# A graph network on one core: first propagation hop as a pass of its own

## The reference

```python
x = _layernorm(x + _L0_gnn_ref(...))   # two mean aggregations over the edges, and an MLP
x = _layernorm(x + _L1_gnn_ref(...))   # a message per edge (edge features), batch norm, SiLU, mean
x = _layernorm(x + _L2_gnn_ref(...))   # h = x @ W + b; out[dst] += h[src] * attention[edge]
x = _layernorm(x + _L3_gnn_ref(...))
# _L3_gnn_ref, K = 3 hops:
deg = segment_sum(ones, dst) + 1;  dinv = rsqrt(deg);  norm = dinv[src] * dinv[dst]
h = x
for _ in range(K):
    h = segment_sum(norm[:, None] * h[src], dst)     # self loops included
return h @ W + b
```

## Time and profile before

| | us |
|---|---|
| median of 3 runs without the profiler | 7859.46 (7859.25 to 7867.06) |
| span of the profiled execution | 9014.9 |
| edge pass of layer 1, first to last gather issue | 1837.5 to 4242.5 |
| attention pass, first to last gather issue | 4774.6 to 7677.3 |
| last block of layer 2 and of the first hop | 7678 to 7788 |
| second hop | 7788 to 8375 |
| third hop and output | 8375 to 9015 |

### The profile page before, as it was taken

One profiled execution on the slowest core, in us unless ns is written; L12 is line 12 of the kernel. 1 busy time (PEld: TensorE's weight loads), 2 busy tenths in 40 slices (PEclk: granted clock), 3 DMA queues, 4 the chain that ended last, 5 costly groups with the idle time before them and its releaser, 6 DMA issues.

```text
span 9014.9 us, 163525 instructions
## 1 busy us (share of the span) xinstructions
PE 5434.1 (60%) x62971; PEld 4715.0 (52%) x62971; DVE 2921.7 (32%) x5181; ACT 1301.5 (14%) x1613; POOL 3562.5 (40%) x3543
## 2 busy tenths in 40 slices
PE   6999889933333333333652455544555455799999
PEld 6999779922222222222542344433444344799998
DVE  6999521111111111112863323332332332311111
ACT  4777510000000000000750000000000000000000
POOL 2111000056666666666725555555555555000000
PEclk9999899966666666666985666666666766899999
DMA  4444268733333332333831222222222222688887
GB/s 129 183 182 182 86 218 254 247 78 81 87 82 81 82 82 76 82 82 98 251 97 35 56 73 73 75 70 70 73 73 74 76 73 76 196 276 268 264 259 229
DMA packets 559779, 1155.29 MB, mean 128 GB/s; under 512 B 155247, under 2 KB 367217, under 8 KB 546465
## 3 DMA queue, kind: packets, MB, share of 16 engines
q1 hardware_dynamic: 234784, 794.54, 27.5%
q10 hardware_dynamic: 215616, 239.17, 8.2%
q0 software_dynamic: 108896, 114.33, 6.5%
HBM read 898.83 MB, written 248.88 MB: 127 GB/s over the span
## 4 chain that ended last, share of the span: by engine, by line
PE 36%; issue 26%; another core or an unknown queue 15%; DVE 5%; ACT 2%; POOL 1%; DVEq 1%; DMA 1%; ACTq 0%; POOLq 0%; SPq 0%; PEldq 0%
PE banks L859 18%; PE banks L953 10%; PE banks L963 5%; POOL gath L366 1%; DVE oneh L1014 1%; DVE area L1836 1%; DVE area L1894 1%; ACT gath L1383 1%; DVE oneh L1845 1%; ACT banks L1380 1%; PE banks L552 1%; PE banks L540 1%; PE banks L1543 1%; PE banks L1552 0%
## 5 line engine op out<-in xcount | busy, mean ns | idle before, releaser
L366 POOL DMA_INDIRECT gath<-tab_l,idx x3328 | 3145.1, 945 | 3296.1 <-DMA idx<-src_idx 1131.6
L1552 PE MATMUL banks<-area,ones 128*128 128x448 f32 (+1 forms) x1040 | 604.9, 752 | 1248.1 <-DVE area L1836 1050.8
L953 PE MATMUL banks<-area 128*128 128x128 f16 x4802 | 575.4, 247 | 894.6 <-issue 893.9
L1552 PEld LDWEIGHTS banks<-area,ones 128*128 128x128 f32 x1040 | 284.5, 285 | 1536.2 <-issue 1522.1
L953 PEld LDWEIGHTS banks<-area 128*128 128x128 fp8e4 x4802 | 356.6, 107 | 1095.2 <-issue 1091.2
L963 PE MATMUL banks<-oneh,gath 128*64 128x128 f32 x3328 | 581.2, 353 | 411.9 <-DMA gath<-tab_l,idx 349.8
L1836 DVE TENSOR_TENSOR area<-gath,banks 128x448 f32<-128x448 f32 (+1 forms) x256 | 138.6, 583 | 1992.2 <-remote 1194.1
L963 PEld LDWEIGHTS banks<-oneh,gath 128*64 128x64 f32 x3328 | 544.7, 188 | 439.0 <-DMA gath<-tab_l,idx 355.6
L825 ACT CAST wide<-banks 128x784 uint16<-128x784 f32 x784 | 651.5, 859 | 221.9 <-PE banks L782 221.9
L794 PE MATMUL banks<-feat,wide 128*128 128x129 f16 x9604 | 670.6, 220 | 0.3 <-ACT wide L825 0.3
L794 PEld LDWEIGHTS banks<-feat,wide 128*128 128x128 fp8e4 x9604 | 606.2, 97 | 0.5 <-issue 0.5
(11 more groups left out here) (257 smaller groups left out, 6169.2 us busy)
## 6 DMA issues: line engine op xcount, KB each, us to landing
gath<-counts SPq DMA_DIRECT2D x294, 784.0 KB, 4.5
oneh<-counts SPq DMA_DIRECT2D x294, 784.0 KB, 4.5
counts<-wide SPq DMA_DIRECT2D x98, 1568.0 KB, 5.2
gath<-counts ACTq DMA_DIRECT2D x98, 784.0 KB
area<-counts ACTq DMA_DIRECT2D x98, 784.0 KB
area<-edge_feat SPq DMA_DIRECT2D x128, 448.0 KB
gath<-tab_l,idx POOLq DMA_INDIRECT x3328
edge_h<-area ACTq DMA_DIRECT2D x128, 416.0 KB
```

What stands on the lines that cost most here:

```text
L366: pool.indirect_dma_start(out=to[:, h, c, 0:H], out_offset=None, in_=table[:, :], in_offset=bass.IndirectOffsetOnAxis(ap=idx[:, slot, c:c ...
L953: last = T.matmul(to, part_in[u].bitcast(f8)[:, t, s * P:(s + 1) * P], block_rows[:, k % 2, s, :, :].rearrange("p a f -> p (a f)"), start= ...
L1552: ins = T.matmul(bank[n][:, 0:(hi - lo) * H], ones[:, :], src[:, lo:hi, :].rearrange("p c f -> p (c f)"), start=first and lo == 0, stop=la ...
```

## The change

The first hop is taken out of the attention pass. Blocks are still normalised during that pass, but step 15 (ACT's copy of `block_rows`) goes: DVE writes the fp16 pair straight into `parts[0]` in steps 13 and 14. After the pass there are no part products; the hops are three dense passes over `counts`: `parts[0]` to `parts[1]`, `parts[1]` to `parts[0]`, and the last one as before from `parts[0]`. SP loads the whole of `counts` once more, in halves of a tile.

```diff
-        L2_STEPS = 15
+        L2_STEPS = 14
-        def part_load(act, b, j):
-...
-            act.dma_start(part_in[j % 2], counts[j * TB:(j + 1) * TB, :, bass.ds(b * BW, BW)]
-                          .rearrange("t p n -> p t n")).then_inc(c_in[j % 2], 16)
-
-        def high_of_block(k):
-            return lambda b, h: V.tensor_copy(block_rows[:, k % 2, :, 0, :], nod[:, h, 0, :, :])
...
+        def high_of_block(b, h):
+            return V.tensor_copy(tiles(parts_of(0, 0), b), nod[:, h, 0, :, :])
+
+        def low_of_block(b, h):
+            return V.tensor_tensor(tiles(parts_of(0, 1), b), nod[:, h, 0, :, :], tiles(parts_of(0, 0), b), ALU.subtract)
...
             hold(act, p_att.added, groups + 2)
-            l2_steps(act, b, [(1, sums_to_sta), *ln_act(4), (11, keep_resid), (15, keep_block(k))])
-            for j in range(NB):
-                if j + 2 < NB:
-                    part_load(act, b, j + 2)
...
+            l2_steps(act, b, [(1, sums_to_sta), *ln_act(4), (11, keep_resid)])
...
-            def step(b, k, st):
+            def step(b, st):
                 if st == 0:
                     l2_steps(pe, b, [(2, feat_by_node)])
-                elif st <= NB // 2:
-                    for j in (2 * st - 2, 2 * st - 1):
-                        part_product(pe, b, k, j)
...
             pe.wait_ge(p_att.summed, GROUPS + RING)
-            pe.sem_inc(h_mm[1], 1)
-            step(EARLY, EARLY, 0)
-            for j in range(NB):
-                part_product(pe, EARLY, EARLY, j, last_block=True)
...
+            pe.sem_inc(h_mm[1], 4)
+            step(EARLY, 0)
+            pe.wait_ge(l_turn, L2_STEPS * NB + 1)
...
-                elif st <= NB // 2:
-                    for j in (2 * st - 2, 2 * st - 1):
-                        part_added(b, j)
...
-            V.memset(sums_a, 0.0).then_inc(s_pre, 1)
-            V.memset(sums_b, 0.0).then_inc(s_pre, 1)
-            dve.wait_ge(s_pre, 9)
...
-                counts_in(sp, 2, each=store_out)
+                counts_in(sp, 2)
+                counts_in(sp, 3, each=store_out)
...
-                times_counts(pe, 1, 1)
+                times_counts(pe, 1, 0)
                 pe.wait_ge(h_dve[0], H_STEPS[0])
+                times_counts(pe, 2, 1)
+                pe.wait_ge(h_dve[1], H_STEPS[1])
...
-                hop_dve(dve, 1, 0)
+                hop_dve(dve, 1, 1)
+                hop_dve(dve, 2, 0)
```

More of the change, by code:

```diff
@@ L925, in keep_block @@
[L925 to L930, removed]
-            hold(act, p_att.added, groups + 2)
-            l2_steps(act, b, [(1, sums_to_sta), *ln_act(4), (11, keep_resid), (15, keep_block(k))])
-            for j in range(NB):
-                if j + 2 < NB:
-                    part_load(act, b, j + 2)
-                if k == EARLY:
-                    act.wait_ge(f_sc, j + 1)
-                    S.copy(tiles(parts_of(1, 0), j), nod[:, j % 2, 0, :, :]).then_inc(f_hi, 1)
@@ L958, in att_group, with early_act @@
+        def low_of_block(b, h):
+            return V.tensor_tensor(tiles(parts_of(0, 1), b), nod[:, h, 0, :, :], tiles(parts_of(0, 0), b), ALU.subtract)
+        def early_act(act, b, groups):
+            hold(act, p_att.added, groups + 2)
+            l2_steps(act, b, [(1, sums_to_sta), *ln_act(4), (11, keep_resid)])
         def att_group(pe, q, k, h):
@@ L983, in early_pe @@
                     att_group(pe, BEFORE + 2 * EACH * i + s, BEFORE // 2 + EACH * i + s // 2, s % 2)
-                    step(2 * i + s // EACH, s // EACH, s % EACH)
+                    step(2 * i + s // EACH, s % EACH)
             for s in range(EACH - 1):
@@ L987, in early_pe @@
                 att_group(pe, q, q // 2, q % 2)
-                step(EARLY - 1, EARLY - 1, s)
+                step(EARLY - 1, s)
             pe.wait_ge(p_att.summed, GROUPS + RING)
-            pe.sem_inc(h_mm[1], 1)
-            step(EARLY, EARLY, 0)
-            for j in range(NB):
-                part_product(pe, EARLY, EARLY, j, last_block=True)
[L995 to L998, removed]
+            pe.sem_inc(h_mm[1], 4)
+            step(EARLY, 0)
+            pe.wait_ge(l_turn, L2_STEPS * NB + 1)
         def early_dve(dve, l2_work):
@@ L1024, in add, with step @@
                     .then_inc(p_att.added, 1)
[L1026 to L1039 removed]
+            def step(b, st):
                 if st == 0:
[L1041 to L1044 removed]
+                    l2_steps(dve, b, [*l2_work, (13, high_of_block), (14, low_of_block)])
             for q in range(2):
                 place(q, q)
[L1049 to L1051 removed]
             with dve.Fori(0, BEFORE // 2) as i:
@@ L1066, in early_dve @@
                     place(q + 2, q % 2)
-                step(EARLY - 1, EARLY - 1, s)
-            step(EARLY, EARLY, 0)
-            def to_parts(j):
-                dve.wait_ge(f_hi, j + 1)
-                V.tensor_tensor(tiles(parts_of(1, 1), j), nod[:, j % 2, 0, :, :], tiles(parts_of(1, 0), j), ALU.subtract)\
-                    .then_inc(f_lo, 1)
-            for j in range(NB):
-                part_added(EARLY, j)
-                dve.wait_ge(c_ev, 2 * (NB * EARLY + j) + 5)
-                if j >= 2:
-                    dve.wait_ge(f_lo, j - 1)
-                V.scalar_tensor_tensor(nod[:, j % 2, 0, :, :], hop_sums(j), 1.0 / COUNT_UNIT, by_tile(dinv2, j), ALU.mult,
-                                       ALU.mult).then_inc(f_sc, 1)
-                if j > 0:
-                    to_parts(j - 1)
-            to_parts(NB - 1)
-        H_STEPS = [8 * TITERS]
+                step(EARLY - 1, s)
+            step(EARLY, 0)
+        H_STEPS = [8 * TITERS] * 2
         def counts_hold(eng):
@@ L1408, in _ @@
                 edges_to_sums_act(n_win, early=True)
-                with act.Fori(0, EARLY // 2) as i:
-                    for k in range(2):
-                        early_act(act, 2 * i + k, k, BEFORE + EACH * (2 * i + k))
-                early_act(act, EARLY - 1, EARLY - 1, BEFORE + EACH * (EARLY - 1))
-                early_act(act, EARLY, EARLY, GROUPS)
+                with act.Fori(0, EARLY) as b:
+                    early_act(act, b, BEFORE + EACH * b)
+                early_act(act, EARLY, GROUPS)
                 turns(act, d_out, [(7, take_feat), *ln_act(10)], LAST_AT.get, DENSE_PERIOD)
@@ L2048, in _ @@
                 dve.wait_ge(s_fold, 3)
[L2049 to L2050 removed]
+                hop_dve(dve, 1, 1)
+                hop_dve(dve, 2, 0)
+                turns(dve, d_out, [(4, both_parts(3)), (5, last_scaled), (9, lambda b, h: add_resid(b, h, 3)),
                                    *ln_dve(10), (16, result_d)], LAST_AT.get, DENSE_PERIOD)
```

32 lines of the change are left out of this document (3 added, 29 removed).

## The result

| | before | after |
|---|---|---|
| median of 4 runs each | 7859.35 (7853.27 to 7867.06) | 8365.92 (8362.46 to 8367.71) |
| ratio, 95% interval | | 1.0642 (1.0627 to 1.0657) |
| span of the profiled execution | 9014.9 | 8362.4 |

The change makes the kernel 506.6 us slower. The forecast was 8371 (8335 to 8405), 5 us off. In the timed runs the time came out as the sum said. But the profile did not: the recorded execution of the changed kernel has a span 1.8 us shorter than its own time of 8364.17, where a span near 9010 was forecast.

A forecast was written before the change was run, and what follows sets the result against it. Timed runs were taken as bound in both gather passes by POOL's unbroken gather stream; 7859.5 + 587.0 (added pass) - 69.9 (last block's parts) - 5.5 (earlier copy), attention pass 0, gave 8371 us, range 8335 to 8405.

The forecast's parts named there:

- The added pass, +587.0: Third dense pass after the attention pass: same work as the present second hop, nothing else beside it, 587.0 us more.
- D: Rival, slower still: PE gets the low clock for all of the new pass, 440 us more, 8811 us; chance 0.02.
- C: Rival, faster: POOL's waits are real and the change removes all, 826.6 us off, 7544 us; chance 0.03.
- The last block's parts, -69.9: Between step 14 and `fold_bias`: the copy and 14 part products of the last block all go, 69.9 us less.
- the copy, -5.5: Before the last block: ACT's copy of step 1 no longer stands behind part loads in its queue, 5.5 us less.
- The attention pass, 0: Part products, additions and loads beside the attention pass's gathers: hidden under the gather stream in timed runs, 0 us gained.
- the account of waits: Both gather passes: POOL's waits of 1155.5 us match profiled span minus timed median, 1155.4, so timed runs lack them.
- PE "near the edge": Attention pass: PE's work per group, 16.1 us at low clock, barely fits under 16.23 us of gathers; 30 us allowed.
- The profiled span, 9012: Profile after the change: attention pass 514.0 us shorter, its remaining waits still there, span 9012 us, nearly as before.
- Rival B: POOL's waits for PE are real in timed runs too; the change gains 514.0 us, 7857 us, no change; chance 0.07.

The follow-up runs named there:

- the repeat: The kernel before, unchanged, profiled a second time in the first batch; it ran in 7870.74 us with a span of 7868.9.
- third recording of before: The kernel before, unchanged, profiled once more in the second batch on another chip; 7864.49 us, span 7862.6.

## Why the prediction was right, and where it was not

**The added pass, +587.0.** 585.4 in the trace, and 588 between the medians with and without it. Nothing lay beside it, as said: DVE 94.8 us, ACT and POOL none. The granted clock of 0.97 rules out D. The timed runs rule out C: they got longer.

**The last block's parts, -69.9; the copy, -5.5.** In sum -75.4; measured from the last gather to the first hop product, 112.5 us in the repeat (6529.33 to 6641.87) and 28.9 after, so -83.6. With the third recording of before (6529.24 to 6636.94, 107.7 us) it is -78.8. The copy's term was right to 0.2 us (6.2 down to 0.5). The other was 2.7 to 7.6 us too small: the parts take 69.9 us in the recording that it was read from the earlier trace rows, and 77.5 and 72.6 in the two others. That is the spread of this stretch, and it can't be put down to the disturbance.

**The attention pass, 0.** 2084.7 down to 2078.6 us, 6 us. Its working counts 98 groups with parts where there are 91, which a term of 0 does not feel. This was the step on which the sign hung, since 514 or 827 us were on offer in the rows, and it held. The reason given was the account of waits: 1155.5 us of them against 1155.4 us between span and median. The reading that such waits are in no timed run is confirmed by the two more recordings and by leaving out, doubling and tripling the parts. That the account closed to 0.1 us was in part luck: it took 2076.1 us for an unbroken pass, and the repeat has 2079.8 and 2084.7, so that by the repeat the two passes were 1143 us too long, and the whole execution 1146.

**PE "near the edge".** The prediction allowed 30 us for real waits, because 16.1 us of PE's work at low clock would just fit under 16.23. The edge was further off: PE is idle for 6.6 us in an undisturbed group, twice the parts still fit, and three times do not. The estimate took the low clock for all of the work; the granted clock rose with it (the table above).

**The profiled span, 9012.** Wrong. The step that failed is the one from "these waits are not in a timed run" to "so they come with the recording": the forecast carried them over to the profile after, with pitch and backlog of the first twelve groups. They belonged to one execution. One of the signs of being wrong did appear, gathers without any wait in the profile after, which the prediction gave to the mechanism of C; it was the wrong reading of that sign, as two recordings of before have none either. With the Trainium skill's "NOTIFIC — the notification-queue block" (section 7.1) the prediction had named full record queues as what may hold up an engine; no run here shows that to be the cause, and two recordings of the same program without waits show that it is not a constant effect of recording. What disturbed the first one is open; neither of the two further recordings brought it back.

**Rival B and its rule.** It had 0.07 and fell with the part products left out. The Trainium skill's "Runtime: NRT & Kernel Launch" (section on the preamble and postamble), which was named beside it, has a gap between profile and reported time that is the same for every kernel. In every run listed here the span is 1.8 to 2.1 us below the time of the same execution (8362.4 and 8364.17; 7868.9 and 7870.74). So that the gap is nearly constant agrees with these runs, but not its size of 6.2 us, nor its sign: the page has the profile's total as the longer of the two. (The span here runs from the first to the last instruction; whether the page's total is the same measure is not shown.) What the prediction had compared was the span of one execution with the times of others. That the 1155.4 us were a longer execution, and no gap between profile and time, is what a constant gap would suggest; the first recording's own time was not among the numbers, so no run shows it.

**The sum against the medians.** Spans of after and of the repeat differ by 493.5 us. By the starts read above: the attention pass begins 12.3 us earlier (4432.35 against 4444.67, behind unchanged code), is 6.1 shorter, what lies between its last gather and the first hop is 83.6 shorter, the pass adds 585.4, the second hop is the same to 0.1 us, and the third hop with the output is 10.2 us longer (650.3 against 640.1). The earlier start is most of why the spans differ by 13 us less than the medians (506.6); it differs between executions of one code, as the changed kernel with two passes has it at 4440.3, and the other undisturbed ones with the same loops up to there between 4437.9 and 4446.6. The last item is in no step of the prediction; it is told below. The forecast missed 10.2 us there and, the other way, 8 us behind the attention pass, 6 in it and 1.6 in the added pass. So it is partly luck that it came within 5 us: these errors have opposite signs.

## What to carry to other kernels

Before anything is read from a profile, compare its span with the timed runs; when they differ by more than a few microseconds, record it again, and do not price a change by the waits of such a profile. Here work beside a stream of gathers cost next to nothing until its engine ran without a gap, and what moved out from under it was paid in full: the first hop cost 6 us beside the gathers (13 of its 14 blocks) and some 80 behind them, and 585 us as a pass. To find out whether work is hidden, leave it out and multiply it; the two together say where the cover ends.

## What the runs showed of the hardware that was not expected

**A branch back on PE.** With the loop closed, PE idles and then runs a slow tile. The price is not a property of the loop alone. Idle times at the first two of five round ends of the third hop, whose code is written alike; first the changed kernel, then the repeat of before:

```profile
7885.59 0.28 PE L1438 MATMUL banks<-wide,ident_h 128*128 x1 [5.24 <-issue]
7978.70 0.28 PE L1438 MATMUL banks<-wide,ident_h 128*128 x1 [5.40 <-issue]
```

```profile
7401.31 0.23 PE L1529 MATMUL banks<-wide,ident_h 128*128 x1 [4.13 <-issue]
7491.42 0.28 PE L1529 MATMUL banks<-wide,ident_h 128*128 x1 [3.52 <-issue]
```

Over all five it is 5.2 to 5.5 us after and 3.5 to 4.1 before, and the idle times add up to 27.0 and 18.9 us, 8.1 of the 10.2 us. The kernel with two passes has the lower ones too (3.5 to 4.2). The kernel with the parts twice has the higher ones (5.1 to 5.5), and this is its third hop's first round end:

```profile
7401.30 0.29 PE L1530 MATMUL banks<-wide,ident_h 128*128 x1 [5.54 <-issue]
```

With the parts three times they are 4.4 to 5.2 us, and the third hop with the output takes 645.3 us. The written code of this loop is alike in all of them, and what stands ahead of it is not; whether its place in memory is the cause was not tried.

**An execution 15% longer than the others.** One recording of the kernel before has a span 1146 and 1152 us longer than the two others. In its gather passes DVE and PE stood idle until "remote" or "issue" in groups like those that the others run without such waits. Its granted clock in the second hop was 0.97, as in the repeat, and that hop took the same 587.0 us; 1143 of the 1146 us lie in the two gather passes.
